# Attention with a mixture of experts on one core: projection and expert products one score tile later in every slot

## Chip, cores and metric

One core of a Trainium2 chip. The metric is the device time of one execution in microseconds (us). The kernel before takes 3419.74 us, the median of three runs (3418.6 to 3422.72).

## What is computed

The reference normalises x (8 x 1024 tokens of 256 values), and adds to it 16-head attention and a mixture of 64 experts, both taken of the normalised tokens:

```python
x = L0_attn_y
xn = _layernorm(x, axis=-1)
x = x + _L0_attn_ref(xn, Wq, bq, Wk, bk, Wv, bv, Wo, bo) \
      + _L0_ffn_ref(xn, router_w, w_gate, w_up, w_down, ws_gate_up, ws_down)
# attention, for each of 8 batches and 16 heads of 64:
att = jnp.einsum('bhqd,bhkd->bhqk', q, k) * scale
att = jax.nn.softmax(att, axis=-1)
out = jnp.einsum('bhqk,bhkd->bhqd', att, v)
# experts: top 8 of 64 by a router, 128 places each, h = silu(g) * u, y = h @ w_down,
# weighted and summed by token; and one shared expert for all tokens
```

## The kernel before

A first stage normalises, routes, makes the values and the shared expert. A last one multiplies by Wo and adds all up. Between them lies the stage of this change: 64 **steps** (NP), one for each pair of heads of each batch, and one for each expert. `run_steps` (L732) writes steps 0 to 2 and 61 to 64 out and runs steps 3 to 60 in a loop in which waits go against register values.

Each engine has its own program, and every step has the same four **slots** (g = 0 to 3). TensorE's program is `step` (L1166):

- Eight score tiles (`score`, L975), here called tile 0 to 7 of the slot: two matmuls each, L988 with `q_full`/`k_full` (128 rows) and L991 with `q_rest`/`k_rest` (65 rows), into a bank of PSUM of 512 columns.
- After some tile a **projection** ("PJ", L1053, six matmuls at L1092), which makes the queries or keys of half the tokens for a later step; it stands in all four slots. After a later tile one **expert item**: "XT" in slot 0 (transposes of the expert's tokens, L1069), "GU" in slot 1 (gate and up products, twelve matmuls, L1077), none in slot 2, "DN" in slot 3 (down product, L1083 and L1084).
- A **quad** (`quad`, L994, four matmuls at L1016), whose maxima give the softmax shift of a later step; in slot 0 the sums (L1046); the products with the values (`pv`, L1021, sixteen matmuls at L1031); a second quad.

ScalarE's program (`step`, L1336) runs in the same order: the exponential of each tile (`exp`, L1278, the instruction is L1289), and at the items' places what empties their banks: for PJ the high part (L1235), for XT a copy (L1239), for GU an exponential and two copies (L1244 to L1246), for DN the weighted copy (L1252). VectorE takes the maxima (L1370) and the low part of each projection (L1380). GpSimd adds the probabilities up (L1633, L1634) and forms the expert's hidden values.

The order of TensorE and ScalarE around the change is the table `ITEMS`: its key n is the number of the tile after which an item stands.

```python
ITEMS = ({2: "PJ", 4: "XT"}, {2: "PJ", 4: "GU"}, {2: "PJ"}, {2: "PJ", 4: "DN"})

for n in range(2 * GROUP):            # eight tiles
    score(s, par, fin, g, n // 2, n % 2)
    if n in ITEMS[g] and present(ITEMS[g][n], g, flags):
        item(s, par, flags, g, ITEMS[g][n])
```

Waits of TensorE that matter here:

- Score tiles go round a **ring** of three banks (RING, L710; `ring_before`, L775). A tile waits until the exponential of the tile three places earlier is done. Tile 4 of slots 1 to 3 is not in the ring (WORK_TILES, L769): it lies in a work bank and waits for VectorE's maxima of the quad before the slot. So tile 3 of a slot waits for the exponential of tile 0 of the same slot. In slots 1 to 3 tiles 5, 6, 7 wait for those of 1, 2, 3.
- PJ waits for the maximum of the first head of the quad before the slot (L1059, `quad_reduced`), in slots 0 and 2 also for the tokens (`x_loaded`, L1061), in slot 0 for the weights (`w_loaded`, L1063).
- The first quad of a slot waits for the low part of the slot's projection (`lows_ready`, L1002), in slot 0 for XT's copy (`xt_copied`, L1006), in slot 1 for GU's copies (`gate_ready`, L1008), in slot 3 for DN's copy (`y_weighted`, L1010).

SyncE issues the DMAs; its waits for `lows_ready` (L1765, L1824, L1835) are behind the projections.

Of the kernel before, what the change touches and what calls it, by code (L numbers as in the profile page):

```python
# [711 lines left out]
SHUFFLES = 12  # L712
QUADS = 4 * SLOTS

ITEMS = ({2: "PJ", 4: "XT"}, {2: "PJ", 4: "GU"}, {2: "PJ"}, {2: "PJ", 4: "DN"})
HAS_ITEM = {"PJ": 3, "XT": 1, "GU": 1, "DN": 1}

FILLERS = (((), (), ("RECIP0", "RECIP1")),
# [24 lines left out]
def present(name, g, flags):  # L743

    return flags[HAS_ITEM[name]]


def is_step(s, n):

    return isinstance(s, int) and s == n  # L750
# [65 lines left out]
def attention_stage(nc, ctx, io, keep):  # L816
# [152 lines left out]
    def _(pe):  # L969
# [5 lines left out]
        def score(s, par, fin, g, i, h):  # L975
            half, kt, j = g // 2, GROUP * (g % 2) + i, 8 * g + 2 * i + h
            out = score_bank(j)
            if j in WORK_TILES:
                pe.wait_ge(quad_reduced, at_most(QUADS * (s + 1) + 4 * g, QUADS * NP))
            else:  # L980
                ring_free(s, USERS.index(j), fin)
            if j == 0:
                if known(s, 1):
                    pe.wait_ge(ones_row, 1)
                pe.wait_ge(placed, DMA * SHUFFLES * (s + 1))
            keys = slice(kt * P, (kt + 1) * P)
            cols = slice(half * HALF, (half + 1) * HALF)
            nc.tensor.matmul(out, k_full[:, par, h, keys], q_full[:, par, h, cols], start=True, stop=False)  # L988
            if g % 2 == 0 and i == 0 and h == 0:
                pe.wait_ge(shift_placed[half], DMA * TURNS * (s + 1))  # L990
            nc.tensor.matmul(out, k_rest[0:DK + 1, par, h, keys], q_rest[0:DK + 1, par, half, h, :],  # L991
                             start=False, stop=True).then_inc(scores_ready, 1)
# [173 lines left out]
        def step(s, par, flags):  # L1166
            fin, att, nxt, prj = flags
            for g in range(SLOTS):
                for n in range(2 * GROUP):
                    if att:  # L1170
# [3 lines that stand above are left out]
                if nxt:  # L1174
# [53 lines left out]
    def _(act):  # L1228
        def item(s, par, g, name):
            if name == "PJ":  # L1230
                which, half = g % 2, g // 2
                if g == 0 and not known(s, 0):
                    act.wait_ge(placed, DMA * SHUFFLES * (s + 1))
                act.wait_ge(pj_filled, 4 * (s + 2) + g + 1)
                nc.scalar.activation(high[:, par, which, half * HALF:(half + 1) * HALF], work[:, 0, :],  # L1235
                                     ACT.Identity, bias=bias[:, par, which:which + 1]).then_inc(highs_ready, 1)
            elif name == "XT":
                act.wait_ge(xt_filled, s + 1)
                nc.scalar.copy(x_et[:].rearrange("p k c -> p (k c)"), work[:, 1, 0:D]).then_inc(xt_copied, 1)  # L1239
            elif name == "GU":  # L1240
                act.wait_ge(gu_filled, s + 1)
                if not known(s, 1):
                    act.wait_ge(hidden_ready, s)
                nc.scalar.activation(silu[:], work[:, 1, P:3 * P], ACT.Exp, scale=-1.0)  # L1244
                nc.scalar.copy(up_gate[:], work[:, 1, 0:3 * P])
                nc.scalar.copy(up_rest[:], work[F2:P, 1, 2 * P:3 * P]).then_inc(gate_ready, 1)  # L1246
            elif name == "DN":
                act.wait_ge(dn_filled, s + 1)
                if not known(s, 2):
                    act.wait_ge(scattered, DMA * (s - 1))  # L1250

                nc.scalar.activation(y_e[:, par, :], work[:, 1, 0:D], ACT.Copy, scale=x_e[:, par, bass.ds(s + D, 1)]  # L1252
                                     ).then_inc(y_weighted, 1)
# [24 lines left out]
        def exp(s, g, i, h):  # L1278
            kt, j = GROUP * (g % 2) + i, 8 * g + 2 * i + h
            act.wait_ge(scores_ready, SCORES * s + j + 1)  # L1280
            if h == 0:
                if i == 0 and not known(4 * s + g - 1, 1):
                    act.wait_ge(pv_done, 4 * s + g - 1)
                added = 14 * s + max(kt, 1) - (0 if g >= 2 else 7)
                if is_step(s, LAST) and g >= 2 and kt > LAST_FIRST:
                    act.wait_ge(last_first, kt - LAST_FIRST)
                elif not known(added, 1):
                    act.wait_ge(sums_added, added)
            nc.scalar.activation(probs[:, kt, h, :], score_bank(j), ACT.Exp, scale=SCALE  # L1289
                                 ).then_inc(probs_ready, 1)  # L1290
# [45 lines left out]
        def step(s, par, flags):  # L1336
            fin, att, nxt, prj = flags
            for g in range(SLOTS):
                for n in range(2 * GROUP):
                    if att:  # L1340
                        exp(s, g, n // 2, n % 2)
                    if n in ITEMS[g] and present(ITEMS[g][n], g, flags):
                        item(s, par, g, ITEMS[g][n])
                    if is_step(s, LAST - 1) and g >= 2 and n % 4 == 3:
# [636 lines left out]
```

## Time and profile before

| What | Value |
|---|---|
| Median of 3 runs | 3419.74 us |
| Profiled execution | 3419.81 us |
| its span, first to last instruction | 3418.1 us |
| TensorE (PE) busy | 3380.4 us, 99% |
| GpSimd (POOL) busy | 2798.8 us, 82% |
| VectorE (DVE) busy | 2515.9 us, 74% |
| ScalarE (ACT) busy | 1658.3 us, 49% |
| mean granted TensorE clock | 0.997 of full speed |

Busy time is the sum of instructions as the profiler saw them. PE is the matmuls, PEld the weight loads that run beside them. Matmuls overlap in the records, so a matmul's start and the start of the next tell more than its duration: PE can be called busy while a start is late.

### The profile page before, as it was taken

To read this page: it belongs to the slowest core of one execution; us is meant where nothing else is said; L and a number is where in the kernel's file an instruction comes from. 1 tells how busy PE (TensorE), PEld (TensorE's weight loads), DVE (VectorE), ACT (ScalarE), POOL (GpSimd) and SP (SyncE) were. 2 spreads that over 40 slices of the span, in tenths; PEclk is the share of its full clock that TensorE was granted. 3 is DMA by queue.
4 is the path that set the end of the run, shared out by engine and by line. 5 is a ranking of instruction groups with operands and counts; after the bars stand their busy time and mean duration, and the time that the engine had idled before them with its cause. 6 is when DMAs were issued, how large, how long until landed. Compare 5 with 4: busy or idle time off the path is not lost.

```text
span 3418.1 us, 61564 instructions
## 1 busy us (share of the span) xinstructions
PE 3380.4 (99%) x16960; PEld 2076.6 (61%) x16960; DVE 2515.9 (74%) x3228; ACT 1658.3 (49%) x3175; POOL 2798.8 (82%) x2381
## 2 busy tenths in 40 slices
PE   8999899999999999999999999999999999999999
PEld 6888555555555555555555555555555555555599
DVE  8999677777777777777777777777777777777776
ACT  5666444444444444444444444444444444444543
POOL 3443499999999999999999999999999999999722
PEclk9999999999999999999999999999999999999999
DMA  7987656777677666667777767776767777766497
GB/s 220 279 257 244 175 145 179 190 186 182 188 184 189 185 184 184 183 182 194 190 185 186 185 183 186 188 183 184 183 179 191 190 187 186 184 186 168 135 354 252
DMA packets 424498, 666.27 MB, mean 195 GB/s; under 512 B 67456, under 2 KB 229120, under 8 KB 424448
## 3 DMA queue, kind: packets, MB, share of 16 engines
q1 hardware_dynamic: 410112, 644.68, 68.0%
q0 software_dynamic: 14336, 20.98, 3.4%
q8 instruction: 24, 0.39, 0.0%
q14 instruction: 26, 0.21, 0.0%
HBM read 305.01 MB, written 125.08 MB: 126 GB/s over the span
## 4 chain that ended last, share of the span: by engine, by line
PE 86%; DVE 1%; POOL 1%; issue 0%; ACT 0%; SPq 0%; DMA 0%; POOLq 0%; DVEq 0%
PE psum L1031 26%; PE psum L988 15%; PE psum L991 14%; PE psum L1092 11%; PE psum L1016 10%; PE psum L1199 5%; PE psum L1077 2%; PE psum L1046 2%; PE psum L1083 1%; PE psum L1084 1%; POOL sums L1634 0%; PE psum L1069 0%; POOL sums L1633 0%; DVE q_rest L1506 0%; DVE merged L1370 0%
## 5 line engine op out<-in xcount | busy, mean ns | idle before, releaser
L1289 ACT ACTIVATE probs<-psum 128x512 f32<-128x512 f32 x2048 | 1077.6, 603 | 1192.5 <-PE psum L991 1185.8
L1370 DVE TENSOR_REDUCE merged<-psum 128x1 fp32r<-128x1024 f32 x1024 | 1201.7, 1215 | 592.0 <-PE psum L1016 571.8
L1633 POOL TENSOR_TENSOR sums<-sums,probs 128x512 f32<-128x512 f32 x761 | 975.3, 1282 | 60.0 <-ACT probs L1289 1.8
L1634 POOL TENSOR_TENSOR sums<-sums,probs 128x512 f32<-128x512 f32 x761 | 976.2, 1283 | 0.0
L1031 PE MATMUL psum<-probs,v_sb 128*64 128x512 f32 x4096 | 935.1, 598 | 0.0
L988 PE MATMUL psum<-q_full,k_full 128*128 128x512 f32 x2048 | 860.9, 420 | 2.5 <-DVE merged L1370 1.6
L991 PE MATMUL psum<-q_rest,k_rest 65*128 65x512 f32 x2048 | 811.0, 396 | 0.0
L1031 PEld LDWEIGHTS psum<-probs,v_sb 128*64 128x64 f32 x4096 | 271.3, 136 | 562.1 <-issue 504.0
L988 PEld LDWEIGHTS psum<-q_full,k_full 128*128 128x128 f32 x2048 | 387.3, 189 | 178.9 <-issue 76.5
L991 PEld LDWEIGHTS psum<-q_rest,k_rest 65*128 65x128 f32 x2048 | 389.2, 190 | 67.2
L1092 PE MATMUL psum<-x_t,w_qk 128*128 128x512 f32 x1536 | 404.7, 399 | 0.7 <-PEq L1941 0.7
L1016 PE MATMUL psum<-high 64*128 64x512 f32 x2016 | 370.1, 445 | 2.9 <-DVE merged L1370 2.9
L1016 PEld LDWEIGHTS psum<-high 64*128 64x128 f32 x2016 | 150.3, 185 | 299.1 <-issue 251.7
L1092 PEld LDWEIGHTS psum<-x_t,w_qk 128*128 128x128 f32 x1536 | 274.8, 189 | 93.7 <-issue 20.4
L1380 DVE SCALAR_TENSOR_TENSOR low<-psum,bias,high 128x512 fp32r<-128x512 f32 x256 | 185.8, 727 | 173.5 <-ACT high L1235 165.0
L1235 ACT ACTIVATE high<-psum,bias 128x512 fp32r<-128x512 f32 x248 | 170.8, 689 | 163.8 <-PE psum L1092 155.1
L1633 POOL TENSOR_TENSOR sums<-probs 128x512 f32<-128x512 f32 x128 | 165.6, 1293 | 91.1 <-ACT probs L1289 89.3
L1399 DVE RECIPROCAL recip<-recip 128x128 f32<-128x128 f32 x256 | 224.3, 918 | 4.8 <-ACT recip L1334 4.8
L1634 POOL TENSOR_TENSOR sums<-probs 128x512 f32<-128x512 f32 x128 | 164.4, 1284 | 0.0
L301 POOL TENSOR_TENSOR xt_low<-xt,xt_high 128x512 fp32r<-128x512 f32 x32 | 40.6, 1289 | 141.5 <-ACT xt L391 141.5
L1416 DVE TENSOR_TENSOR out_raw<-out_raw,sum_all 128x512 f32<-128x512 f32 x128 | 149.6, 1169 | 3.1 <-DMA sum_all<-recip 3.1
L1664 POOL TENSOR_TENSOR probs<-probs 128x1024 f32<-128x1024 f32 x16 | 44.2, 2760 | 127.9 <-DMA probs<-moe 127.9
(164 smaller groups left out, 3385.0 us busy)
## 6 DMA issues: line engine op xcount, KB each, us to landing
x_t<-xt SPq DMA_DIRECT2D x118, 1024.0 KB, 6.9
k_full<-high SPq DMA_DIRECT2D x256, 256.0 KB
v<-values SPq DMA_DIRECT2D x64, 512.0 KB, 3.4
w_qk<-wqk_parts SPq DMA_DIRECT2D x64, 512.0 KB
v_sb<-v SPq DMA_DIRECT2D x64, 512.0 KB, 5.4
q_full<-high SPq DMA_DIRECT2D x128, 256.0 KB
q_full<-low SPq DMA_DIRECT2D x128, 256.0 KB
k_rest<-low SPq DMA_DIRECT2D x128, 256.0 KB
```

Of the source, the lines that this page charges most:

```text
L988: nc.tensor.matmul(out, k_full[:, par, h, keys], q_full[:, par, h, cols], start=True, stop=False)
L991: nc.tensor.matmul(out, k_rest[0:DK + 1, par, h, keys], q_rest[0:DK + 1, par, half, h, :], start=False, stop=True).then_inc(scores_ready, 1)
L1016: last = nc.tensor.matmul(work[:, 2 * h + part, :], high[rows, 1 - par, 0, q * P:(q + 1) * P], high[rows, 1 - par, 1, part * HALF:(part + ...
L1031: last = nc.tensor.matmul(out_ps[rows, :], v_sb[:, par, kt, rows], probs[:, kt, h, :], start=(kt == 0), stop=(kt == KT - 1))
L1092: last = nc.tensor.matmul(out, w_qk[:, par, which, wp, kd, :], x_t[:, xp, kd, cols], start=(j == 0 and kd == 0), stop=(j == 2 and kd == KD ...
L1199: last = nc.tensor.matmul(out, ot(par, o, batch)[:, h, k * P:(k + 1) * P], wo[:, w, batch * BATCH + h, :], start=(n == 0), stop=(n == 3 * ...
L1289: nc.scalar.activation(probs[:, kt, h, :], score_bank(j), ACT.Exp, scale=SCALE).then_inc(probs_ready, 1)
L1370: nc.vector.tensor_reduce(out=merged[:, q // GROUP, col:col + 1], in_=work[:, 2 * h:2 * h + 2, :].rearrange("p b c -> p (b c)"), axis=AX, ...
L1380: nc.vector.scalar_tensor_tensor(out=low[:, par, which, cols], in0=bank, scalar=bias[:, par, which:which + 1], in1=f32(high[:, par, which, ...
L1399: nc.vector.reciprocal(recip[:, cols], recip[:, cols]).then_inc(recip_ready, 1)
L1633: nc.gpsimd.tensor_tensor(total[:, 0, :], first[:, 0, :], probs[:, kt, 0, :], ALU.add)
L1634: nc.gpsimd.tensor_tensor(total[:, 1, :], first[:, 1, :], probs[:, kt, 1, :], ALU.add).then_inc(sums_added, 1)
```

## The change

In every slot PJ stands one tile later (after tile 3, the fourth), and XT, GU and DN too (after tile 5, the sixth), on TensorE and on ScalarE. Nothing else is changed.

```diff
@@ -712,7 +712,7 @@
-ITEMS = ({2: "PJ", 4: "XT"}, {2: "PJ", 4: "GU"}, {2: "PJ"}, {2: "PJ", 4: "DN"})
+ITEMS = ({3: "PJ", 5: "XT"}, {3: "PJ", 5: "GU"}, {3: "PJ"}, {3: "PJ", 5: "DN"})
```

## Rows read from the trace of the kernel before

**Rows 1.** The page: engines, GpSimd in 40 slices, the chain that ended last

```profile
PE 3380.4 (99%) x16960; PEld 2076.6 (61%) x16960; DVE 2515.9 (74%) x3228; ACT 1658.3 (49%) x3175; POOL 2798.8 (82%) x2381
...
POOL 3443499999999999999999999999999999999722
...
PE 86%; DVE 1%; POOL 1%; issue 0%; ACT 0%; SPq 0%; DMA 0%; POOLq 0%; DVEq 0%
```

**Rows 2.** Groups by line; behind the bar idle time before them

```profile
L988 PE MATMUL psum<-q_full,k_full 128*128 128x512 f32 x2048 | 860.9, 420 | 2.5 <-DVE merged L1370 1.6 <-DVE low L1380 0.9
...
L1016 PE MATMUL psum<-high 64*128 64x512 f32 x2016 | 370.1, 445 | 2.9 <-DVE merged L1370 2.9
```

**Rows 3.** Timeline, PE, step 25, slot 1: start us, us

```profile
1511.66 0.40 PE L991 MATMUL psum<-q_rest,k_rest 65*128 65x512 f32 x1
1511.90 1.55 PE L1092 MATMUL psum<-x_t,w_qk 128*128 128x512 f32 x6
1513.29 0.39 PE L988 MATMUL psum<-q_full,k_full 128*128 128x512 f32 x1
```

**Rows 4.** Timeline, PE and PEld, step 25, slot 0, around PJ

```profile
1500.07 0.39 PE L991 MATMUL psum<-q_rest,k_rest 65*128 65x512 f32 x1
1500.35 1.22 PEld L1092 LDWEIGHTS psum<-x_t,w_qk 128*128 128x128 f32 x6 [0.32 <-issue]
...
1501.85 0.39 PE L988 MATMUL psum<-q_full,k_full 128*128 128x512 f32 x1
```

**Rows 5.** Timeline, ACT, step 25: exponential of tile 0, slots 0 to 3

```profile
1499.74 0.60 ACT L1289 ACTIVATE probs<-psum 128x512 f32<-128x512 f32 x1 [5.02 <-PE psum L991]
...
1511.24 0.60 ACT L1289 ACTIVATE probs<-psum 128x512 f32<-128x512 f32 x1 [4.30 <-PE psum L991]
...
1522.89 0.60 ACT L1289 ACTIVATE probs<-psum 128x512 f32<-128x512 f32 x1 [4.50 <-PE psum L991]
...
1533.12 0.60 ACT L1289 ACTIVATE probs<-psum 128x512 f32<-128x512 f32 x1 [4.93 <-PE psum L991]
```

**Rows 6.** Timeline, PE, step 25: last matmul of tile 2, slots 2 and 3

```profile
1523.24 0.40 PE L991 MATMUL psum<-q_rest,k_rest 65*128 65x512 f32 x1
...
1533.47 0.40 PE L991 MATMUL psum<-q_rest,k_rest 65*128 65x512 f32 x1
```

**Rows 7.** Timeline, step 62 (no projection), slot 0: tile 0's exponential, tile 3

```profile
3146.71 0.60 ACT L1289 ACTIVATE probs<-psum 128x512 f32<-128x512 f32 x1 [4.94 <-PE psum L991]
...
3147.36 0.19 PEld L988 LDWEIGHTS psum<-q_full,k_full 128*128 128x128 f32 x1 [0.18 <-ACT probs L1289]
...
3147.21 0.39 PE L991 MATMUL psum<-q_rest,k_rest 65*128 65x512 f32 x1
3147.44 0.41 PE L988 MATMUL psum<-q_full,k_full 128*128 128x512 f32 x1
3147.70 0.39 PE L991 MATMUL psum<-q_rest,k_rest 65*128 65x512 f32 x1
```

**Rows 8.** Timeline, step 25, slot 1: GU's last copy, the quad

```profile
1516.53 0.26 ACT L1246 COPY up_rest_e<-psum 64x128 f32<-64x128 f32 x1
...
1517.06 0.73 PE L1016 MATMUL psum<-high 64*128 64x512 f32 x4
```

**Rows 9.** Timeline, step 25, slot 0: XT's copy, the quad

```profile
1503.59 0.38 ACT L1239 COPY x_et<-psum 128x256 f32<-128x256 f32 x1
...
1504.49 0.73 PE L1016 MATMUL psum<-high 64*128 64x512 f32 x4
```

**Rows 10.** Timeline, step 25: slot 2's low part and quad, slot 3's DN copy and quad

```profile
1525.79 0.75 DVE L1380 SCALAR_TENSOR_TENSOR low<-psum,bias,high 128x512 fp32r<-128x512 f32 x1
...
1527.29 0.73 PE L1016 MATMUL psum<-high 64*128 64x512 f32 x4
...
1537.28 0.47 ACT L1252 ACTIVATE y_e<-psum,x_e 128x256 f32<-128x256 f32 x1 [0.32 <-PE psum L1084]
...
1538.39 0.73 PE L1016 MATMUL psum<-high 64*128 64x512 f32 x4
```

## The prediction

> **What bounds the kernel now.** I began with the page. TensorE is busy 99% of the span and makes up 86% of the chain that ended last [rows 1]: whatever delays it lengthens the kernel, and only taking a delay from it can shorten the kernel. The groups by line come next, for what it still waits for: the idle time before all 2048 L988 matmuls is 2.5 us, before the 2016 of the quads 2.9 us [rows 2]. But the records overlap, so a late start need not show as idle time. I therefore read the timeline of one step of the loop (step 25) from start to start. In slot 1 the last matmul of tile 2 starts at 1511.66 and tile 3 follows behind the projection at 1513.29: seven starts in 1.63 us, 0.233 us each, with no delay [rows 3]. The same stretch in slot 0 takes from 1500.07 to 1501.85, 1.78 us: 0.15 us are lost, because the projection's first weight load starts 0.28 us after tile 2's last matmul instead of at once [rows 4]. By the code that load waits for a maximum and for two DMAs. This is the one delay of the loop that the change can take away.
>
> **What is moved.** TensorE and ScalarE run the same instructions; no DMA is in the items, and none is moved. A tile takes 2 x 0.233 = 0.47 us of TensorE. Relative to the tiles and the quad around them the projection and the expert item come 0.47 us later. Tile 4 still stands behind four tiles and the projection, so its wait for VectorE's maxima is where it was. Two things differ: tile 3 is at once behind tile 2, and everything that an item must hand back before the quad has 0.47 us less.
>
> **Tile 3 behind tile 0's exponential.** The projection used to stand between them and hid the ring's wait. What such a wait costs shows in two places. In step 62, which has no projection, tile 3 already follows tile 2. Tile 0's exponential ends at 3146.71 + 0.60 = 3147.31, the load starts at 3147.36, so a release reaches a load in 0.05 us. The load is 0.15 us behind tile 2's last matmul (3147.21), and the matmul behind it at 3147.70 is 0.49 after that one where two starts take 0.47: 0.02 us lost [rows 7]. The other place is slot 0's projection: 0.28 us late, 0.15 lost [rows 4]. Both fit lateness less 0.13 us, and I take that.
>
> In the loop the exponential comes later than in step 62. Its end, less the start of tile 2's last matmul, is 1500.34 - 1500.07 = 0.27 in slot 0, 1511.84 - 1511.66 = 0.18 in slot 1, 1523.49 - 1523.24 = 0.25 in slot 2, and 1533.72 - 1533.47 = 0.25 in slot 3 [rows 3 to 6]. With 0.05 for the release and less 0.13: 0.19, 0.10, 0.17 and 0.17, together **0.63 us a step**. Slot 0's old loss goes, since the maximum has 0.47 us more and the projection itself is pushed back: **-0.15 us**. Bounds for the 0.63: 0.08 (4 x 0.02, as in step 62, if the loop's exponential were that early) and 1.15 (the four latenesses of 0.32, 0.23, 0.30, 0.30 in full). I take 0.63, as it follows from two measured points and this step's own ends.
>
> One rule of the notes speaks for less. The Trainium skill, page "TensorE: Matmul & The Clock Gate", section "The mechanism", says that a weight load overlaps matmuls in flight only when it goes to other row groups. Then a full load would start behind the matmul before it in any case, and a late release would cost only what it exceeds 0.233 us by: 0.09, 0, 0.07, 0.07. The rows of slot 1 speak against it: if a load of 0.19 us had to wait for the matmul before it, full-height matmuls could not start every 0.233 us [rows 3, 7]. The sum by that rule would be 0.40 us a step less.
>
> **GU's copies in front of slot 1's quad.** The last copy ends at 1516.79 and the quad starts at 1517.06, 0.27 us later [rows 8]. ScalarE has finished tile 5's exponential before GU's products are done, so its three instructions still follow the products directly, and all of them move by 0.47 us against the quad: they would end 0.20 us behind its due time. To that comes the release. A load with its own wait needs 0.05 us [rows 7]; here the wait stands in an instruction in front of the load's, so I take twice that, 0.10 us (an estimate). **0.30 us a step.** Bounds: 0.25 (release 0.05) and 0.47 (if the whole 0.27 is the shortest way).
>
> **XT's copy in front of slot 0's quad.** It ends at 1503.97, the quad starts at 1504.49, 0.52 us later [rows 9]. Less 0.47 leaves 0.05, less 0.10 for the release: **0.05 us a step**, bounds 0 and 0.22.
>
> **The rest at nothing.** DN's copy ends at 1537.75, 0.64 us before its quad at 1538.39, which leaves 0.17 us against 0.10 needed; slot 2's low part ends at 1526.54, 0.75 us before the quad at 1527.29, which leaves 0.28 [rows 10]. Bounds for both together 0 and 0.10 (should a release take 0.27 us at DN). The reciprocals behind that low part push VectorE's maxima back by at most as much; the slot's second quad, behind all sixteen matmuls of the values, is the first to wait for them. SyncE's transfers behind the low parts are for later steps. GpSimd is busy nine tenths of nearly every slice of the loop [rows 1], but what it waits for, the exponentials of tile 3, comes earlier, so it gets slack.
>
> **Sum.** 0.63 - 0.15 + 0.30 + 0.05 = 0.83 us a step. The 58 steps of the loop (3 to 60): 48.1 us. The four steps with projections outside it, taken with exponentials as early as in step 62: 0.35 each, 1.4 us; step 62 has GU and its quad, 0.3 us. Together 49.8 us on the profiled execution's 3419.8 us (span 3418.1), which lies within 0.1 us of the median: 3469.6, told as 3469.
>
> **The rivals.** A measurement of this kernel can tell about 0.2% (6.8 us) from no change.
> - *The release is slow.* If 0.27 us [rows 8] is the shortest way from a copy to a quad, slots 0, 1 and 3 lose 0.17, 0.17 and 0.10 more: 0.44 x 62 = 27 us, 3496. Against it stands step 62's 0.05 [rows 7]. A middle value (0.15) gives about 3476. Chance of over 3488: 0.08.
> - *Late loads cost less,* as by that rule of the skill: 0.43 us a step, 0.43 x 58 + 1.7 = 27 us, 3446. The rows speak against it. 0.08.
> - *No loss at tile 3 and none at the quads; slot 0's projection gains.* This ends faster: 0.15 x 58 = 9 us, 3411. It decides at a load 0.13 us behind tile 2's last matmul, so exponentials would have to end within 0.08 us of its start, where the rows have 0.18 to 0.27 [rows 4 to 6], and GU's release would have to overlap the quad. 0.03.
> - *TensorE takes it back,* or the loss at the quad and the gain nearly cancel (0.15 against a ring loss of 0.08 as in step 62 and a quad loss near 0.1): within 6.8 us of 3420. The first and last steps show that early exponentials exist. 0.03.
> - *The forecast,* 3452 to 3488: 0.78.
>
> **How the numbers follow.** 3469 is the likeliest case. Its range from the bounds: tile 3 between 0.45 and 0.75, GU 0.25 to 0.40, XT 0 to 0.15, which is 0.55 to 1.15 us a step and 34 to 68 us; 3452 to 3488 leaves out 0.08 above and 0.14 below. Faster 0.03, same 0.03, slower 0.94.
>
> **What would show it.** Right: in the loop, tile 3's load starts 0.05 us behind the end of tile 0's exponential, 0.2 to 0.3 us behind tile 2's last matmul; the waits list names the exponential (L1289) before L988's loads some 230 times; slot 0's projection starts at 0.233 us without a delay; slot 1's quad starts about 0.1 us behind L1246's end; a step of the loop takes about 0.8 us longer. Wrong: a tile 3 that starts on time, a quad of slot 1 whose distance to L1246 is still 0.27 us, or a step that is longer by less than 0.4 us.

## The result

| | Median us | Runs | Ratio to before, 95% interval |
|---|---|---|---|
| before | 3420.64 | 4 (3418.6 to 3422.72) | |
| after | 3478.66 | 4 (3477.26 to 3479.51) | 1.017, 1.0154 to 1.0185 |

The change costs 58.0 us. The forecast was 49 us (3469, range 3452 to 3488).

The page of the kernel after, the lines that answer to [rows 1]:

```profile
span 3475.5 us, 61564 instructions
...
PE 3417.7 (98%) x16960; PEld 2078.0 (60%) x16960; DVE 2533.7 (73%) x3228; ACT 1658.6 (48%) x3175; POOL 2822.8 (81%) x2381
...
PE 85%; DVE 2%; POOL 1%; issue 1%; ACT 0%; DMA 0%; SPq 0%; POOLq 0%; DVEq 0%
```

The span is 57.4 us longer, and TensorE's busy time grew by 37.3 us with the same matmuls: part of a late start is booked as a longer matmul. The share of busy time hides most of the loss. The list of waits names one place (us in total, times, longest us):

```profile
PEld psum L988 <- ACT probs L1289: 71.2, 233, 0.4
```

Almost all of these loads are tile 3's: in the kernel before there are 14 such waits, none of them in the loop. The 233 come near 4 x 58 = 232 by chance, though. In the loop it is tile 3 of slots 0, 1 and 3 in all 58 steps, but tile 3 of slot 2 in 29 of them only; in the other 29 the same wait is put down to "issue". The remaining 30 lie in the steps outside the loop. The 71.2 us are idle time of the load path and not what TensorE lost.

**Tile 3.** Step 30 of the kernel after, slot 0 (exponential, then the load, then the matmuls; each kind from the timeline of its engine):

```profile
1748.83 0.60 ACT L1289 ACTIVATE probs<-psum 128x512 f32<-128x512 f32 x1 [5.02 <-PE psum L991]
...
1749.48 0.19 PEld L988 LDWEIGHTS psum<-q_full,k_full 128*128 128x128 f32 x1 [0.35 <-ACT probs L1289]
...
1749.17 0.39 PE L991 MATMUL psum<-q_rest,k_rest 65*128 65x512 f32 x1
1749.48 0.50 PE L988 MATMUL psum<-q_full,k_full 128*128 128x512 f32 x1
1749.82 0.40 PE L991 MATMUL psum<-q_rest,k_rest 65*128 65x512 f32 x1
1750.06 1.32 PE L1092 MATMUL psum<-x_t,w_qk 128*128 128x512 f32 x5
```

The exponential ends at 1749.43, the load starts 0.05 us later, 0.31 behind tile 2's last matmul. The second matmul of tile 3 starts 1749.82 - 1749.17 = 0.65 us after that one, where two starts took 0.47: 0.18 us lost. The projection follows at 0.24 without a delay, so slot 0's old 0.15 us [rows 4] is gone. Slot 2 of the same step loses 0.17 (1773.46 - 1772.82 less 0.47):

```profile
1772.82 0.39 PE L991 MATMUL psum<-q_rest,k_rest 65*128 65x512 f32 x1
1773.12 0.50 PE L988 MATMUL psum<-q_full,k_full 128*128 128x512 f32 x1
1773.46 0.40 PE L991 MATMUL psum<-q_rest,k_rest 65*128 65x512 f32 x1
```

**The quads.** In slot 1, GU's last copy and the quad, with the last tile's last matmul ahead of it (ACT, then PE and the loads):

```profile
1766.27 0.26 ACT L1246 COPY up_rest_e<-psum 64x128 f32<-64x128 f32 x1
...
1766.02 0.40 PE L991 MATMUL psum<-q_rest,k_rest 65*128 65x512 f32 x1
1766.64 0.73 PE L1016 MATMUL psum<-high 64*128 64x512 f32 x4 [0.22 <-issue]
...
1766.61 0.33 PEld L1016 LDWEIGHTS psum<-high 64*128 64x128 f32 x4 [0.63 <-issue]
```

The copy ends at 1766.53 and the load starts 0.08 us later. From the last tile's matmul to the quad it is 0.62 us; before, this way was 1516.74 to 1517.06 [rows 8], 0.32 us. 0.30 us lost, as forecast. Slot 0's way grew from 0.33 us (1504.16 to 1504.49 [rows 9]) to 0.36. The last tiles of the two slots in the kernel before:

```profile
1504.16 0.40 PE L991 MATMUL psum<-q_rest,k_rest 65*128 65x512 f32 x1
...
1516.74 0.39 PE L991 MATMUL psum<-q_rest,k_rest 65*128 65x512 f32 x1
```

and slot 0 after:

```profile
1753.30 0.40 PE L991 MATMUL psum<-q_rest,k_rest 65*128 65x512 f32 x1
1753.66 0.73 PE L1016 MATMUL psum<-high 64*128 64x512 f32 x4
```

Slot 2 was forecast free of loss. It isn't (VectorE, GpSimd, TensorE):

```profile
1774.33 0.69 DVE L1416 TENSOR_TENSOR out_raw<-out_raw,sum_all 128x512 f32<-128x512 f32 x1
1774.94 1.38 DVE L1422 TENSOR_SCALAR silu_e<-silu_e 128x256 f32<-128x256 f32 x1
1776.24 0.74 DVE L1380 SCALAR_TENSOR_TENSOR low<-psum,bias,high 128x512 fp32r<-128x512 f32 x1
...
1774.61 1.56 POOL L1633 TENSOR_TENSOR sums<-probs 128x512 f32<-128x512 f32 x1 [1.34 <-ACT probs L1289]
...
1776.72 0.39 PE L991 MATMUL psum<-q_rest,k_rest 65*128 65x512 f32 x1
1777.22 0.73 PE L1016 MATMUL psum<-high 64*128 64x512 f32 x4
```

The quad starts 0.50 us behind the last tile's last matmul, 0.18 too late. The low part, which ends at 1776.98, began late, because VectorE's addition for the silu ahead of it (L1422) took 1.38 us. In the kernel before it is short, and the groups by line say it for all 64, first before, then after:

```profile
L1422 DVE TENSOR_SCALAR silu_e<-silu_e 128x256 f32<-128x256 f32 x64 | 19.5, 305 | 4.0 <-ACT up_rest_e L1246 4.0
```

```profile
L1422 DVE TENSOR_SCALAR silu_e<-silu_e 128x256 f32<-128x256 f32 x64 | 85.7, 1339 | 4.4 <-ACT up_rest_e L1246 4.4
```

What differs is GpSimd. Its first sum of the second half waits for tile 3's exponential, and that now comes earlier. So the sum starts at 1774.61, ahead of the addition, and the addition ends 0.15 us behind the sum's end (1776.32 and 1776.17). The sum itself takes 1.56 us instead of 1.28: it starts while VectorE's product of two tiles (L1416) runs, and ends as if it had begun when that product was nearly done.

Slot 3 was forecast free of loss too, and is: its way from the last tile to the quad, with DN's copy in front, is 0.32 us.

```profile
1788.16 0.39 PE L991 MATMUL psum<-q_rest,k_rest 65*128 65x512 f32 x1
1788.48 0.73 PE L1016 MATMUL psum<-high 64*128 64x512 f32 x4
```

**All steps.** The steps shown are typical. The same distances from start to start, as means over the 58 steps of the loop, before and after (us):

| | Slot 0 | Slot 1 | Slot 2 | Slot 3 |
|---|---|---|---|---|
| lost at tile 3 | 0 to 0.19 | 0 to 0.09 | 0 to 0.17 | 0 to 0.17 |
| last tile to the first quad | 0.33 to 0.36 | 0.32 to 0.62 | 0.32 to 0.50 | 0.33 to 0.32 |
| the whole slot | 11.61 to 11.68 | 11.58 to 11.97 | 10.23 to 10.59 | 11.10 to 11.25 |

Tile 3 loses 0.63 us a step, the quads 0.51, and slot 0's projection gains 0.15. A step takes 45.49 us instead of 44.52: 0.98 x 58 = 56.6 of the 57.4 us.

### The profile page after: what moved, and what is told of

Same layout as the page of the kernel before. It is cut to its first block, busy times and chain, and to the rows that moved or that the text cites. A ratio compares the mean times of both kernels' runs of the same rounds, so it can differ in the third digit from the quotient of the medians.

```text
span 3475.5 us, 61564 instructions
## 1 busy us (share of the span) xinstructions
PE 3417.7 (98%) x16960; PEld 2078.0 (60%) x16960; DVE 2533.7 (73%) x3228; ACT 1658.6 (48%) x3175; POOL 2822.8 (81%) x2381
## 4 chain that ended last, share of the span: by engine, by line
PE 85%; DVE 2%; POOL 1%; issue 1%; ACT 0%; DMA 0%; SPq 0%; POOLq 0%; DVEq 0%
PE psum L1031 25%; PE psum L988 16%; PE psum L991 13%; PE psum L1092 10%; PE psum L1016 10%; PE psum L1199 5%; PE psum L1077 2%; PE psum L1046 2%; PE psum L1083 1%; PE psum L1084 1%; POOL sums L1634 1%; POOL sums L1633 1%; PE psum L1069 0%; DVE q_rest L1506 0%; DVE merged L1370 0%
## 5 line engine op out<-in xcount | busy, mean ns | idle before, releaser
L988 PE MATMUL psum<-q_full,k_full 128*128 128x512 f32 x2048 | 884.0, 432 | 2.0 <-DVE merged L1370 1.1
L1092 PEld LDWEIGHTS psum<-x_t,w_qk 128*128 128x128 f32 x1536 | 289.9, 189 | 69.3 <-issue 2.2
L1633 POOL TENSOR_TENSOR sums<-probs 128x512 f32<-128x512 f32 x128 | 182.7, 1427 | 84.8 <-ACT probs L1289 83.1
L1634 POOL TENSOR_TENSOR sums<-probs 128x512 f32<-128x512 f32 x128 | 167.5, 1309 | 0.0
L609 PE MATMUL psum<-wv,xt_high 128*128 128x512 f32 x512 | 140.1, 395 | 0.0
```

What stands on the lines that cost most here:

```text
L1092: last = nc.tensor.matmul(out, w_qk[:, par, which, wp, kd, :], x_t[:, xp, kd, cols], start=(j == 0 and kd == 0), stop=(j == 2 and kd == KD ...
L1633: nc.gpsimd.tensor_tensor(total[:, 0, :], first[:, 0, :], probs[:, kt, 0, :], ALU.add)
L1634: nc.gpsimd.tensor_tensor(total[:, 1, :], first[:, 1, :], probs[:, kt, 1, :], ALU.add).then_inc(sums_added, 1)
```

## The experiments

Theory: four losses a step (tile 3 behind tile 0's exponential in every slot; GU's and XT's copies; slot 2's quad through GpSimd and VectorE) and one gain. Rivals: the losses belong to one part alone; tile 3's delay is not from the exponential; VectorE is late for a reason of its own. The medians of the kernel before beside the runs are 3420.68 us for experiments 1 to 4, 3420.21 for 5 to 8 and 3419.41 for 9 to 11; differences to the changed kernel are to its 3478.66 us.

**1. The projection alone**

```diff
-ITEMS = ({3: "PJ", 5: "XT"}, {3: "PJ", 5: "GU"}, {3: "PJ"}, {3: "PJ", 5: "DN"})
+ITEMS = ({3: "PJ", 4: "XT"}, {3: "PJ", 4: "GU"}, {3: "PJ"}, {3: "PJ", 4: "DN"})
```

> Only the projection stands one tile later; XT, GU and DN stay behind the fifth tile. Theory (from the trace after): tile 3 loses 0.61 us a step in the loop, slot 0's old 0.144 us goes, and slot 2's quad loses 0.17 us because VectorE's silu addition (L1422) runs beside GpSimd's sums: 0.64 x 58 = 37 us, so about 3457 us; slot 1's quad has no delay. Rival (the loss at slot 2's quad comes of the items, or all losses are the items'): 3447 or less.

Measured: 3457.91 us (ratio to before 1.0111, 1.0094 to 1.0128). Two thirds of the loss are the projection's, slot 2's included.

**2. The expert items alone**

```diff
-ITEMS = ({3: "PJ", 5: "XT"}, {3: "PJ", 5: "GU"}, {3: "PJ"}, {3: "PJ", 5: "DN"})
+ITEMS = ({2: "PJ", 5: "XT"}, {2: "PJ", 5: "GU"}, {2: "PJ"}, {2: "PJ", 5: "DN"})
```

> Only XT, GU and DN stand one tile later; the projection stays behind the third. Theory: slot 1's quad loses 0.30 us and slot 0's 0.04 us a step, tile 3 and slot 2 nothing, slot 0's projection still loses its 0.144: 0.34 x 62 = 21 us, about 3441 us. Rival (the quad's loss needs the later projection too, or ScalarE's exponentials in front of the copies): 3420 to 3430 us.

Measured: 3445.99 us (1.0076, 1.0059 to 1.0092), 5 us more than expected. These 5 us are not in the loop: in the profiled execution its 58 steps take 2603.1 us where they take 2582.0 before, 21.2 more, as expected. The other 5 us of the span lie outside it, where TensorE's granted clock is at half (1.2 GHz) for 27.5 us instead of 20.7; half of these 6.8 us would be 3.4 (an estimate), and the rest is open. The two parts cost 37.2 and 25.3 us, together 62.5 where the whole costs 58.0. By the loop alone it is 39.5 and 21.2, together 60.7 for 56.6: nearly independent, with 4 us that stay open.

**3. GpSimd held back**

```diff
                 for kt in range(1, KT):
...
+                    if half == 1 and kt == 1:
+                        pool.wait_ge(silu_vec, 3 * s + 1)
                     pool.wait_ge(probs_ready, SCORES * s + 16 * half + 2 * kt + 2)
```

> The changed kernel, with one wait more: GpSimd's first sum of the second half waits until VectorE's silu addition (L1422) is done. Theory (the two share something, so that the addition takes 1.38 us instead of 0.29 and makes the low part late): L1422 is back at 0.3 us, slot 2's quad starts without a delay, 0.17 x 58 = 10 us less than the changed kernel, about 3469 us. Rival (VectorE is late for another reason, or the later sums cost elsewhere): 3478 us or more.

Measured: 3468.27 us (1.014, 1.0123 to 1.0157), 10.4 us less than the changed kernel. The timeline of slot 2 in step 30 (VectorE, GpSimd, TensorE; the held sum's line is now L1635):

```profile
1772.40 0.29 DVE L1422 TENSOR_SCALAR silu_e<-silu_e 128x256 f32<-128x256 f32 x1
1773.45 0.75 DVE L1380 SCALAR_TENSOR_TENSOR low<-psum,bias,high 128x512 fp32r<-128x512 f32 x1 [0.76 <-ACT high L1235]
...
1772.91 1.29 POOL L1635 TENSOR_TENSOR sums<-probs 128x512 f32<-128x512 f32 x1 [2.17 <-DVE silu_e L1422]
...
1774.17 0.39 PE L991 MATMUL psum<-q_rest,k_rest 65*128 65x512 f32 x1
1774.49 0.73 PE L1016 MATMUL psum<-high 64*128 64x512 f32 x4
```

The addition is back at 0.29 us, the low part waits for the high part again and not for VectorE, and the quad is 0.32 us behind the last tile, which is also slot 2's mean over the loop (0.50 in the changed kernel). A wait more on an engine that is busy over 80% of the span makes the kernel faster: shown is that the addition is slow because GpSimd's sum runs, and that this was the whole of slot 2's loss.

**4. ScalarE's wait for the tile last**

```diff
         def exp(s, g, i, h):
             kt, j = GROUP * (g % 2) + i, 8 * g + 2 * i + h
-            act.wait_ge(scores_ready, SCORES * s + j + 1)
             if h == 0:
...
                     act.wait_ge(sums_added, added)
+            act.wait_ge(scores_ready, SCORES * s + j + 1)
```

> The changed kernel, but ScalarE waits for the score tile last, behind the waits for the values' products and for the sums, which are met long before. Theory (tile 0's exponential starts late because two more waits are taken after the tile is there): it starts 0.04 us behind the tile instead of 0.11 to 0.20, tile 3 loses 0.02 instead of 0.15 us a slot, 0.54 x 58 = 31 us less than the changed kernel, about 3447 us. Rival (the exponential's start is bound by something else, or tile 3's delay is not from it): 3478 us.

Measured: 3457.29 us (1.0109, 1.0093 to 1.0126), 21 us less, not 31. Tile 3 did what was expected, here in slot 2 of step 30: the load is 0.15 us behind tile 2's last matmul at 1763.05.

```profile
1762.55 0.60 ACT L1289 ACTIVATE probs<-psum 128x512 f32<-128x512 f32 x1 [4.67 <-PE psum L991]
...
1763.20 0.19 PEld L988 LDWEIGHTS psum<-q_full,k_full 128*128 128x128 f32 x1 [0.19 <-ACT probs L1289]
```

But slot 2 gained nothing by it, because its quad waits for the low part, and that did not move:

```profile
1764.70 1.71 POOL L1633 TENSOR_TENSOR sums<-probs 128x512 f32<-128x512 f32 x1 [1.18 <-ACT probs L1289]
...
1764.57 0.69 DVE L1416 TENSOR_TENSOR out_raw<-out_raw,sum_all 128x512 f32<-128x512 f32 x1
1765.18 1.38 DVE L1422 TENSOR_SCALAR silu_e<-silu_e 128x256 f32<-128x256 f32 x1
1766.48 0.74 DVE L1380 SCALAR_TENSOR_TENSOR low<-psum,bias,high 128x512 fp32r<-128x512 f32 x1
...
1766.79 0.39 PE L991 MATMUL psum<-q_rest,k_rest 65*128 65x512 f32 x1
1767.46 0.73 PE L1016 MATMUL psum<-high 64*128 64x512 f32 x4 [0.28 <-DVE low L1380]
```

The quad is 0.67 us behind the last tile instead of 0.50: 0.17 x 58 = 10 us, what is missing from the 31. The expectation of experiment 5 puts this down to a collision that lasts longer. The rows do not show that. The sum does start earlier and is recorded at 1.71 us instead of 1.56, but the addition takes the same 1.38 us. Behind slot 2's first score matmul the sum ends at 4.63 us, the addition at 4.78 and the low part at 5.44 in both kernels (medians of the 58 steps). What changed is the last tile, which is 0.15 us earlier, so that the way to the quad reads longer; the slot takes 10.59 us in both. In these two kernels the sum is there before L1416 ends, and how long before makes no difference to VectorE.

**5. Both cures** (the edits of 3 and 4 together)

> The changed kernel with both cures: ScalarE's wait for the tile last, and GpSimd's second half held until the silu addition is done. In exp_order tile 3 was at 0.15 us behind tile 2 as wanted, but the quad of slot 2 began 0.15 us later still. Theory (that was GpSimd starting still earlier and meeting the silu addition for longer): with the hold both gains come in full, 0.54 + 0.18 = 0.72 x 58 = 42 us less than the changed kernel, about 3437 us. Rival (the quad of slot 2 is late by itself): 3447 us or more.

Measured: 3439.15 us (1.0055, 1.0039 to 1.007), 39.5 us less than the changed kernel; in the loop it is 41.9. With the hold the low part is no longer late, so tile 3's gain comes in full in slot 2 too: the way from the last tile to the quad is 0.32 us there, where experiment 4 has 0.66 (means of the 58 steps).

**6. The low part's wait last among the quad's**

```diff
             if q % 2 == 0:
-                if prj:
-                    pe.wait_ge(lows_ready, 4 * (s + 2) + g + 1)
...
                 pe.wait_ge(quad_reduced, QUADS * (s + 1) + 2 * q)
+            if q % 2 == 0 and prj:
+                pe.wait_ge(lows_ready, 4 * (s + 2) + g + 1)
```

> The changed kernel, but TensorE takes the wait for the low part last of the quad's waits. Theory (in slot 2 the low part needs 0.21 us to reach the quad because two more waits are taken behind it): the way shrinks to 0.05 to 0.07 us, slot 2's quad loses 0.03 instead of 0.18 us, 0.14 x 58 = 8 us less, about 3470 us. Rival (the 0.21 us is the way of any release to a quad): 3478 us.

Measured: 3480.29 us (1.0173, 1.0157 to 1.0188), no gain. Slot 2 was cured: its low part ends at 1780.78 + 0.74 = 1781.52 and the quad starts at 1781.57, 0.35 behind the last tile (1781.22). But the wait for the copies now has two waits behind it instead of one. In slot 1 the last copy ends at 1770.97 and the quad starts only 0.19 us later, where it was 0.11:

```profile
1770.71 0.26 ACT L1246 COPY up_rest_e<-psum 64x128 f32<-64x128 f32 x1
...
1771.16 0.73 PE L1016 MATMUL psum<-high 64*128 64x512 f32 x4 [0.31 <-issue]
```

Slot 0's quad, which waits for XT's copy, is later by as much: 0.46 us behind the last tile instead of 0.36 (means). One order served all four slots, and each slot's last release is another one. The rival fell for slot 2, but the forecast of the total failed, because I had looked at one slot.

**7. The silu addition behind the low part**

```diff
-           (("NORM0", "SILU0"), ("SILU1", "SILU2"), ("NORM1",)),
+           (("NORM0",), ("SILU0", "SILU1", "SILU2"), ("NORM1",)),
```

> The changed kernel, but VectorE's silu addition stands behind the low part in slot 2. Theory (the addition is slow, but it only hurts because the low part waits behind it): the low part starts 0.03 us behind the high part, slot 2's first quad has no delay, about 3469 us, as with GpSimd held; the addition stays at 1 us or more. Rival (the later reciprocals push the maxima back so far that the second quad waits): 3475 us or more.

Measured: 3618.86 us (1.0577, 1.0561 to 1.0593), 140 us slower than the changed kernel and the worst miss. The low part is on time, yet everything behind it is not:

```profile
1846.61 0.92 DVE L1422 TENSOR_SCALAR silu_e<-silu_e 128x256 f32<-128x256 f32 x1
1847.56 1.76 DVE L1426 RECIPROCAL silu_e<-silu_e 128x128 f32<-128x128 f32 x2
1849.24 2.29 DVE L1370 TENSOR_REDUCE merged<-psum 128x1 fp32r<-128x1024 f32 x2
1851.44 3.17 DVE L1416 TENSOR_TENSOR out_raw<-out_raw,sum_all 128x512 f32<-128x512 f32 x1
...
1851.54 1.28 POOL L1633 TENSOR_TENSOR sums<-sums,probs 128x512 f32<-128x512 f32 x1
...
1855.81 2.42 PE L1092 MATMUL psum<-x_t,w_qk 128*128 128x512 f32 x5 [1.25 <-DVE merged L1370]
```

The normalisation behind the maxima (L1416) meets GpSimd's next sums and takes 3.17 us, where the same instruction takes 0.68 in the changed kernel (and 1.64 before); the maxima behind it hold slot 3's projection, which starts 1.65 us behind tile 3 (1854.16). The rival had the direction, not the size.

Part of the 140 us is TensorE's clock. Its mean is 0.986 here and 0.998 in the changed kernel: in 22 of the 58 steps the granted clock falls to 0.5 (1.2 GHz) for a while behind this wait, and in the last row above the five matmuls take 2.42 us, where five take 1.32 in the row under **Tile 3**. Steps with such a fall take 48.77 us, the others 47.18: 22 x 1.59 = 35 us. No other kernel here has half clock in its loop.

**8. The kernel before, slot 0's projection with the maximum's wait last**

```diff
                 if known(s, 0) and 4 * (s + 2) + g > 0:
                     pe.wait_ge(lows_ready, 4 * (s + 2) + g)
-                if nxt and not known(reduced - 1, 1):
-                    pe.wait_ge(quad_reduced, reduced - 1)
                 if which == 0:
                     pe.wait_ge(x_loaded[half], DMA * x_loads(s + 2))
                 if g == 0:
                     pe.wait_ge(w_loaded, 2 * DMA * (s + 3))
+                if nxt and not known(reduced - 1, 1):
+                    pe.wait_ge(quad_reduced, reduced - 1)
```

> The kernel before, but slot 0's projection takes the wait for VectorE's maximum last, behind those for tokens and weights. Theory (its load was 0.28 us late because two more waits are taken after the maximum is there): the load starts about 0.1 us behind tile 2's last matmul, nothing is lost, 0.144 x 58 = 8 us less than before, about 3412 us. Rival (the maximum itself is too late): 3420 us.

Measured: 3412.09 us (0.9973, 0.9962 to 0.9984). The load is 0.10 us behind tile 2's last matmul, and seven starts take 1719.24 to 1720.85, 1.61 us, where [rows 4] has 1.78:

```profile
1719.34 0.55 PEld L1092 LDWEIGHTS psum<-x_t,w_qk 128*128 128x128 f32 x3
...
1719.24 0.39 PE L991 MATMUL psum<-q_rest,k_rest 65*128 65x512 f32 x1
1719.47 1.54 PE L1092 MATMUL psum<-x_t,w_qk 128*128 128x512 f32 x6
1720.85 0.39 PE L988 MATMUL psum<-q_full,k_full 128*128 128x512 f32 x1
```

This beats both kernels.

**9. Control: ScalarE's new order in the kernel before** (the edit of 4)

> Control: the kernel before, with ScalarE's wait for the tile last. Theory (tile 0's exponential matters only where tile 3 stands right behind tile 2): no change, 3420 us within 3. Rival (earlier exponentials help or hurt by themselves, so that exp_order measured them and not tile 3): more than 7 us off.

Measured: 3421.13 us (1.0004, 0.9995 to 1.0013). No change: what experiment 4 gained is tile 3's wait.

**10. The kernel before with the edits of 4 and 8**

> The kernel before with both new orders of waits (ScalarE's tile last, slot 0's projection's maximum last). Theory: only the second counts, 3412 us. Rival (more waits were hidden behind each other): under 3408 us.

Measured: 3411.77 us (0.9979, 0.997 to 0.9988), the same as 8.

**11. The projection later in slot 0 alone**

```diff
-ITEMS = ({2: "PJ", 4: "XT"}, {2: "PJ", 4: "GU"}, {2: "PJ"}, {2: "PJ", 4: "DN"})
+ITEMS = ({3: "PJ", 4: "XT"}, {2: "PJ", 4: "GU"}, {2: "PJ"}, {2: "PJ", 4: "DN"})
```

with the edit of 4.

> The kernel before with ScalarE's wait for the tile last and the projection one tile later in slot 0 alone. Theory: the projection no longer waits for the maximum (0.144 us gained), tile 3 loses 0.02 us: 0.12 x 58 = 7 us less than before, about 3413 us. Rival (moving the projection costs more than tile 3's wait): 3420 us or more.

Measured: 3412.64 us (0.998, 0.9971 to 0.9989). The move gains 0.12 us a step (0.15 less tile 3's 0.02) where tile 3's wait is nearly free and the expert item stays in its place; only in one slot of four was there something to gain.

**The loop alone.** The parts outside the loop differ between these kernels by some us, so the 58 steps in the profiled executions tell an effect better than the total (us, from step 3's first score matmul to step 61's):

| | Loop | Difference | Expected |
|---|---|---|---|
| before | 2582.0 | | |
| changed | 2638.6 | +56.6 to before | +48 |
| 1, projection | 2621.5 | +39.5 to before | +37 |
| 2, items | 2603.1 | +21.2 to before | +21 |
| 3, GpSimd held | 2627.1 | -11.5 to changed | -10 |
| 4, ScalarE's order | 2616.5 | -22.0 to changed | -31 |
| 5, both | 2596.7 | -41.9 to changed | -42 |
| 6, low part's wait last | 2640.8 | +2.2 to changed | -8 |
| 7, addition behind | 2771.6 | +133.0 to changed | -10 |
| 8, projection's order | 2573.7 | -8.3 to before | -8 |
| 9, control | 2582.1 | +0.1 to before | 0 |
| 10, 4 and 8 | 2572.6 | -9.4 to before | -8 |
| 11, slot 0 | 2574.3 | -7.6 to before | -7 |

## Why the prediction was right, and where it was short

- *TensorE bounds, and a late start need not show as idle time.* Right: 57.4 us of span, 37.3 of them inside busy time.
- *Tile 3, 0.63 us a step.* Right, slot by slot: 0.19, 0.09, 0.17 and 0.17 us for the forecast 0.19, 0.10, 0.17 and 0.17, and the rule of lateness less 0.13 held again. Experiments 4, 5 and 9 tie it to tile 0's exponential. One sign came true by luck: the waits list has 233 entries for the "some 230", but 203 of them are the ones meant.
- *The rule that a load overlaps only matmuls of other row groups* (the Trainium skill, "TensorE: Matmul & The Clock Gate", "The mechanism"). The runs disagree for these loads: by it a load 0.31 us late would have cost 0.08 us, and it cost 0.18. The prediction left out that the same section also lets a load go ahead of matmuls in flight when it targets the background weight buffer. That would fit the rows; no run here shows which buffer a load takes.
- *Slot 0's old loss, -0.15.* Right. Experiments 8 and 11 get it by itself, 8.1 and 6.8 us.
- *GU, 0.30.* Right: 0.30, with a release of 0.08 us for the 0.10 taken. The rival of a 0.27 us release is out: here the quad starts 0.11 us behind the copy.
- *XT, 0.05.* 0.03 in the step shown and on average.
- *Slot 2's low part at nothing.* This step failed, and it is the difference between 49 and 58 us: 0.18 x 58 = 10 us, and experiment 3 measured 10.4. The range held because it was wide enough for a term that was not in it. Two things were wrong in the step. I took the low part's start as bound by the high part alone and said that GpSimd "gets slack" because tile 3's exponential comes earlier; that earlier start was the cause, since the sum then stands ahead of VectorE's addition, which takes 1.38 us instead of 0.29. And I took 0.10 us for every release, where the low part's, with more waits behind it, takes 0.21 (1776.98 to the quad's load at 1777.19); with the 0.28 us left and the low part on time, the 0.21 would still have fitted, as experiment 3 shows.
- *DN at nothing.* Right: slot 3's way to its quad is 0.33 us before and 0.32 after. In experiment 2, where DN alone moves in slot 3, the slot is not longer either (11.10 and 11.09 us).

With the missed term the sum is 0.83 + 0.18 = 1.01 us a step for 0.98 measured, and 58 of them and the 1.7 us outside the loop make 60 us for the 57.4 measured (56.6 in the loop, 0.8 outside).

## What to carry to other kernels

An item between two tiles of a ring also covers the wait of the second; before moving it, take the time from the release to the next load, and do it for each slot. Where a change gives an engine off the critical path its input earlier, look up what the engines beside it run at that new time. In a list of waits put the one that is met last at the end, and check which one that is in every place that shares the code. And when a way from A to B grows, check whether B came later or A earlier (experiment 4).

## What the runs showed of the hardware

- A weight load released late costs its lateness behind the start of the matmul before, less about 0.13 us: 0.15 late cost 0.02 (step 62 before, and all slots of experiment 4), 0.22 cost 0.09, 0.28 cost 0.15, 0.30 cost 0.17, 0.31 cost 0.18.
- The last wait ahead of a load needs 0.05 us from the release (1749.43 to 1749.48). Waits standing behind the released one add to that: with one behind it the load came 0.08 us after the release (slot 1's copy, 1766.53 to 1766.61), with two 0.18 and 0.21. In experiment 6 the wait for the copy in slot 1 got a second wait behind it, and the way to the quad's matmul grew from 0.11 to 0.19 us; slot 2's wait for the low part lost the two behind it, and its way shrank from 0.24 (1776.98 to 1777.22) to 0.05.
- A 128x256 VectorE addition with a constant, 0.29 us by itself, took 1.38 us when a GpSimd sum was under way, and ended 0.15 us behind it, however early the sum had started (1.38 in experiment 4 too); a 128x512 product of two tiles of SBUF (L1416) took 3.17 in experiment 7, through two GpSimd sums in a row, where 0.68 us is its time without. This agrees with the Trainium skill, page "SBUF — State Buffer", section "SBUF: two separate sides": the pair of ports that the two engines share is locked for a whole instruction, and the other waits in full. The page says it of a VectorE instruction with two inputs in SBUF, as L1416, or in a mode that uses two ports; no run here shows in which mode the addition ran, and that an instruction stays out through two sums in a row is seen here only.
